# A DLRM interaction tower on one core: 27-vector products in two visits a step, and a second table of 1,250 rows on chip

## What is computed

```python
e = stack([tbl_f[ids[:, f]] for f in range(26)], axis=1)
combined = concatenate([dense[:, None, :], e], axis=1)
interactions = einsum('bnd,bmd->bnm', combined, combined)[:, TRIU_I, TRIU_J]
h = concatenate([dense, interactions, dense], axis=1)
h = maximum(h @ W_top1 + b_top1, 0.0)
h = maximum(h @ W_top2 + b_top2, 0.0)
y = h @ W_top3
```

## Time and profile before

| | us |
|---|---|
| median of 3 runs | 372.38 |
| lowest and highest | 370.5, 372.94 |
| span of the profiled execution | 373.1 |
| PE busy in it | 332.0 (89%) |
| PE weight loads busy | 298.5 (80%) |
| POOL busy | 258.6 (69%) |
| DVE busy, ACT busy | 207.1, 188.8 |

### The profile page before, as it was taken

The page is one execution under the profiler, slowest core; times in us unless marked ns, Lnnn a source line. Parts: engine busy times, 40 slices in busy tenths (PEclk is TensorE's granted clock), DMA queues, the critical chain, the costliest instruction groups (busy, mean ns, idle before and its releaser), DMA issues.

```text
span 373.1 us, 13491 instructions
## 1 busy us (share of the span) xinstructions
PE 332.0 (89%) x6048; PEld 298.5 (80%) x6048; DVE 207.1 (55%) x375; ACT 188.8 (51%) x223; POOL 258.6 (69%) x280
## 2 busy tenths in 40 slices
PE   0377859899999899998999999999999999999895
PEld 0377848898799778996789978998799878997685
DVE  3799745694089703874059912885079704860030
ACT  2698462455545473553635564554645563556402
POOL 6777777777777777777777777777777777776000
PEclk9997898899999999998999999999999999999999
DMA  7999426772226622464215722464226622442230
GB/s 178 246 259 212 135 79 174 193 229 69 55 68 151 198 53 59 95 194 125 58 54 128 233 54 58 93 192 131 58 59 150 205 54 57 105 116 62 51 40 21
DMA packets 49332, 44.24 MB, mean 119 GB/s; under 512 B 33359, under 2 KB 39094, under 8 KB 49274
## 3 DMA queue, kind: packets, MB, share of 16 engines
q1 hardware_dynamic: 39166, 25.36, 26.9%
q0 software_dynamic: 8704, 17.84, 18.2%
q10 hardware_dynamic: 1404, 0.17, 0.3%
HBM read 37.91 MB, written 5.44 MB: 116 GB/s over the span
## 4 chain that ended last, share of the span: by engine, by line
PE 82%; DMA 5%; issue 5%; ACT 4%; DVE 2%; SPq 1%; ACTq 1%; DVEq 0%
PE banks L443 38%; PE banks L462 14%; PE mlp L481 13%; PE moved L426 8%; PE mlp L491 7%; DMA w_sb<-in_tbl_dram 3%; DVE masks L672 1%; ACT vectors L818 1%; ACT hidden L846 1%; PE mlp L502 1%; SPq L250 1%; ACTq L229 1%; DMA scratch<-products 1%; DMA features<-scratch 1%; DVE low L659 1%
## 5 line engine op out<-in xcount | busy, mean ns | idle before, releaser
L401 POOL DMA_INDIRECT rows<-in_tbl_dram,ids_sb x272 | 257.7, 948 | 84.0 <-issue 80.8
L672 DVE TENSOR_TENSOR masks<-hot_ids,row_of 125x512 fp32r<-125x512 int32 (+1 forms) x336 | 185.6, 619 | 93.7 <-PE banks L443 84.8
L443 PE MATMUL banks<-masks,high 125*128 125x256 f32 x592 | 154.3, 298 | 17.4 <-DVE low L659 17.4
L443 PE MATMUL banks<-masks,low 125*128 125x256 f32 x592 | 150.3, 291 | 0.0
L443 PEld LDWEIGHTS banks<-masks,high 125*128 125x128 f32 x592 | 118.9, 201 | 18.1 <-issue 15.2
L443 PEld LDWEIGHTS banks<-masks,low 125*128 125x128 f32 x592 | 119.1, 201 | 0.0
L818 ACT ACTIVATE vectors<-moved 128x512 f32<-128x512 f32 (+1 forms) x80 | 86.8, 1085 | 4.6 <-PE moved L426 4.3
L801 ACT ACTIVATE vectors<-banks 128x512 f32<-128x512 f32 (+1 forms) x40 | 44.4, 1111 | 77.4 <-PE banks L443 77.4
L462 PEld LDWEIGHTS banks<-vectors 128*27 128x27 f32 x4096 | 44.5, 104 | 24.7 <-issue 19.6
L462 PE MATMUL banks<-vectors 128*27 128x27 f32 x4096 | 54.1, 193 | 9.7 <-issue 5.0
L481 PE MATMUL mlp<-features,w_sb 117*128 117x256 f32 x224 | 54.6, 388 | 0.0
(11 more groups left out here) (46 smaller groups left out, 64.4 us busy)
## 6 DMA issues: line engine op xcount, KB each, us to landing
hot_ids<-in_ids_of_field_dram SPq DMA_DIRECT2D x32, 256.0 KB, 4.9
rows<-in_tbl_dram,ids_sb POOLq DMA_INDIRECT x272
features<-scratch SPq DMA_DIRECT2D x7, 351.0 KB
scratch<-products SPq DMA_DIRECT2D x56, 42.2 KB
scratch<-products SPq DMA_DIRECT2D x28, 81.2 KB
w_sb<-in_tbl_dram SPq DMA_DIRECT2D x3, 448.0 KB
hot_ids<-in_ids_of_field_dram SPq DMA_DIRECT2D x8, 128.0 KB
dense_sb<-in_dense_dram SPq DMA_DIRECT2D x8, 128.0 KB, 5.2
```

The costliest lines, as they stand in the source:

```text
L401: pool.indirect_dma_start(rows[:, (tile * TILE_ROWS + v) % RING, :], None, tables[f][:, :], bass.IndirectOffsetOnAxis(ap=ids_sb[:, tile, f ...
L443: last = nc.tensor.matmul(banks[:, j % BANKS, m * CHUNK:(m + 1) * CHUNK], part[:, part_of(j * PAIR + m, k), :], masks[:, mask % MASK_RING, ...
L672: nc.vector.tensor_tensor(masks[:, mask % MASK_RING, 0:size], hot_ids[0:PART_ROWS, n % ID_RING, 0:size], row_of[0:PART_ROWS, row:row + 1]. ...
```

## The change

**Two visits a step.** The 64 matmuls of a `multiply` step are done as two groups of 32 with other work between them, in all steps but the first two of chunk 0 and the last of chunk 7. In `end_of_chunk` the first step's second group comes after the second `first_layer`, and the second step is spread around the third `first_layer` and the fourth turn; the `keep_step` calls on ScalarE move with them. The third and the fourth step are laced with the first look-up of the next chunk.

**A second table of 1,250 rows.** Field 3 (`SOMETIMES`) is put on chip too. In chunks 5 and 7 it is looked up, as the second table of the pair j = 4; in the other six chunks it is gathered as before, as the batch of one row. So chunks 5 and 7 have 16 gathers a tile and no fifth batch. Its table has its own staging buffer, `last_table`, loaded on SP after the ids. It is rounded, copied and split after the other nine (`round_table(HOT)`, `copy_table(HOT)`, `split(HOT)`).

```diff
+LOOKED_UP = (5, 7)
+ONE_HOT = [SOMETIMES, ALWAYS] + SHORTS
+STAGED = SHORTS + [ALWAYS, SOMETIMES]
...
+def batches_of(t):
+    return TILE_BATCHES - (t // TILES in LOOKED_UP)
+def fields_of(c, j):
+    if j < HOT_PAIRS - 1:
+        return (PAIR * j, PAIR * j + 1)
+    return (HOT, HOT - 1) if c in LOOKED_UP else (HOT - 1,)
...
             load_ids(1, slice(TILES, ALL_TILES))
+            load_table(HOT)
...
-                for b in range(TILE_BATCHES):
+                for b in range(batches_of(tile)):
                     gather(tile, b)
...
+            def multiply(c, s, visits=range(VISITS)):
+                for visit in visits:
+                    multiply_part(c, s, visit)
...
-                for g in range(STEP_GROUPS):
+                for g in range(visit * VISIT_GROUPS, (visit + 1) * VISIT_GROUPS):
...
-                last.then_inc(step_ready, 1)
+                if visit == VISITS - 1:
+                    last.then_inc(step_ready, 1)
...
             def end():
-                multiply(LAST, 2)
-                second_layer(LAST - 1, 1)
+                multiply(LAST, 2, (0,))
+                second_layer(LAST - 1, 1, range(0, 2))
+                multiply(LAST, 2, (1,))
+                second_layer(LAST - 1, 1, range(2, MTILES1))
                 multiply(LAST, 3)
...
             def end_of_chunk(i):
                 first_layer(i - 1, 0)
-                multiply(i, 0)
+                multiply(i, 0, (0,))
                 turn(b, 0)
                 first_layer(i - 1, 1)
-                multiply(i, 1)
+                multiply(i, 0, (1,))
                 turn(b, 1)
                 first_layer(i - 1, 2)
+                multiply(i, 1, (0,))
                 turn(b, 2)
                 first_layer(i - 1, 3)
                 turn(b, 3)
+                multiply(i, 1, (1,))
                 second_layer(i - 1, 0)
                 turn(b, 4)
                 if i < LAST:
                     second_layer(i - 1, 1)
-                    multiply(i, 2)
-                    look_up(i + 1, 0)
-                    multiply(i, 3)
+                    multiply(i, 2, (0,))
+                    look_up(i + 1, 0, range(0, 3))
+                    multiply(i, 2, (1,))
+                    look_up(i + 1, 0, range(3, 5))
+                    multiply(i, 3, (0,))
+                    look_up(i + 1, 0, range(5, PARTS[0]))
+                    multiply(i, 3, (1,))
...
@@ VectorE
             make_masks(0, HOT_PAIRS - 1)
+            split(HOT)
             place_dense(0)
...
@@ ScalarE, first_chunk
                 keep_batch(1, 1)
+                round_table(HOT)
+                copy_table(HOT)
                 keep_step(0, 0)
...
@@ ScalarE, end_of_chunk
                 keep_first(i - 1, 0)
-                keep_step(i, 0)
                 keep_batch(b, 0)
                 keep_first(i - 1, 1)
-                keep_step(i, 1)
+                keep_step(i, 0)
                 keep_batch(b, 1)
                 keep_first(i - 1, 2)
                 keep_batch(b, 2)
                 keep_first(i - 1, 3)
                 keep_batch(b, 3)
+                keep_step(i, 1)
                 keep_second(i - 1, 0)
```

More of the change, by code:

```diff
@@ L11 @@
 SHORT, LONG = 1000, 1250
-LONGS = [f for f in range(FIELDS) if ROWS[f] == LONG][:1]
-ONE_HOT = [f for f in range(FIELDS) if ROWS[f] == SHORT] + LONGS
+SHORTS = [f for f in range(FIELDS) if ROWS[f] == SHORT]
+ALWAYS, SOMETIMES = [f for f in range(FIELDS) if ROWS[f] == LONG][:2]
+LOOKED_UP = (5, 7)
+ONE_HOT = [SOMETIMES, ALWAYS] + SHORTS
+STAGED = SHORTS + [ALWAYS, SOMETIMES]
 GATHERED = [f for f in range(FIELDS) if f not in ONE_HOT]
@@ L36 @@
 CHUNK_STEPS = TILES * TILE_STEPS
+VISITS = 2
+VISIT_GROUPS = STEP_GROUPS // VISITS
 BATCH_SIZES = (4, 4, 4, 4, 1)
-TILE_ROWS = len(GATHERED)
+TILE_ROWS = len(GATHERED) + 1
 TILE_BATCHES = len(BATCH_SIZES)
-assert sum(BATCH_SIZES) == TILE_ROWS
+assert sum(BATCH_SIZES) == TILE_ROWS and BATCH_SIZES[-1] == 1
 CHUNK_BATCHES = TILES * TILE_BATCHES
@@ L50 @@
 PAIR = BANK // CHUNK
-HOT = len(ONE_HOT)
+HOT = len(STAGED) - 1
 HOT_PAIRS = -(-HOT // PAIR)
 WIDTHS = [min(PAIR, HOT - PAIR * j) for j in range(HOT_PAIRS)]
-PARTS = [ROWS[ONE_HOT[PAIR * j]] // PART_ROWS for j in range(HOT_PAIRS)]
+PARTS = [ROWS[STAGED[PAIR * j]] // PART_ROWS for j in range(HOT_PAIRS)]
 FIRST_PART = [sum(WIDTHS[n] * PARTS[n] for n in range(j)) for j in range(HOT_PAIRS + 1)]
@@ L64 @@
 assert CHUNK_STEPS == BANKS
[L65 removed]
+KINDS = [ROWS[SHORT_] // PART_ROWS for SHORT_ in (STAGED[0], STAGED[-1])]
 HIDDEN1, HIDDEN2 = 512, 256
@@ L85, with batches_before, rows_before @@
 SCRATCH_DMAS = QUAD_DMAS * QUADS
+def batches_of(t):
+    return TILE_BATCHES - (t // TILES in LOOKED_UP)
+def batches_before(t):
+    return sum(batches_of(n) for n in range(t))
+def rows_before(t):
+    return sum(TILE_ROWS - (n // TILES in LOOKED_UP) for n in range(t))
+def fields_of(c, j):
+    if j < HOT_PAIRS - 1:
+        return (PAIR * j, PAIR * j + 1)
+    return (HOT, HOT - 1) if c in LOOKED_UP else (HOT - 1,)
 def tile_batch(b):
@@ L94, in batch_of_row @@
 def batch_of_row(g):
-    tile, v = divmod(g, TILE_ROWS)
-    return tile * TILE_BATCHES + max(b for b in range(TILE_BATCHES) if tile_batch(b)[0] <= v)
+    tile = max(t for t in range(ALL_TILES) if rows_before(t) <= g)
+    v = g - rows_before(tile)
+    return batches_before(tile) + max(b for b in range(TILE_BATCHES) if tile_batch(b)[0] <= v)
 def part_of(h, k):
@@ L170, in build @@
         dense_loaded = [sem(f"dense_loaded{n}") for n in range(2)]
-        table_loaded = [sem(f"table_loaded{n}") for n in range(HOT)]
+        table_loaded = [sem(f"table_loaded{n}") for n in range(HOT + 1)]
         weights_loaded = sem("weights_loaded")
@@ L419, in turn @@
                     return
-                n = t * TILE_BATCHES + b
+                if b >= batches_of(t):
+                    return
+                n = batches_before(t) + b
                 batch = tile_batch(b)
-                pe.wait_ge(rows_loaded[t % TILES * TILE_BATCHES + b], (t // TILES + 1) * 16 * len(batch))
+                loads = sum(b < batches_of(n) for n in range(t % TILES, t + 1, TILES))
+                pe.wait_ge(rows_loaded[t % TILES * TILE_BATCHES + b], loads * 16 * len(batch))
                 if n:
@@ L426, in turn, with look_up @@
                     last = nc.tensor.transpose(moved[:, m * TILE:(m + 1) * TILE],
-                                               rows[:, (t * TILE_ROWS + v) % RING, :], identity[:, :])
+                                               rows[:, (rows_before(t) + v) % RING, :], identity[:, :])
                 last.then_inc(batch_ready, 1)
-            def look_up(c, j):
+            def look_up(c, j, ks=None):
+                ks = ks or range(PARTS[j])
+                if c == min(LOOKED_UP) and j == HOT_PAIRS - 1:
+                    pe.wait_ge(low_made, HOT + 1)
@@ L431, in look_up @@
                 if c == 0:
                     pe.wait_ge(low_made, PAIR * j + WIDTHS[j])
-                elif j < BANKS:
+                elif j < BANKS and ks[0] == 0:
                     pe.wait_ge(step_kept, (c - 1) * CHUNK_STEPS + j + 1)
-                if j >= BANKS:
+                if j >= BANKS and ks[0] == 0:
                     pe.wait_ge(pair_kept, c * HOT_PAIRS + j - BANKS + 1)
-                for k in range(PARTS[j]):
+                for k in ks:
                     mask = c * MASKS + FIRST_MASK[j] + k
@@ L440, in look_up @@
                     pe.wait_ge(mask_made, mask + 1)
-                    for m in range(WIDTHS[j]):
+                    fields = fields_of(c, j)
+                    for m, h in enumerate(fields):
                         for part in (high, low):
-                            last = nc.tensor.matmul(banks[:, j % BANKS, m * CHUNK:(m + 1) * CHUNK], part[:, part_of(j * PAIR + m, k), :],
+                            last = nc.tensor.matmul(banks[:, j % BANKS, m * CHUNK:(m + 1) * CHUNK], part[:, part_of(h, k), :],
@@ L489, in second_layer @@
                     pe.wait_ge(first_kept, MTILES1 * (c + 1))
-                for k in range(MTILES1):
+                for k in ks:
                     last = nc.tensor.matmul(mlp[:, m, 0:CHUNK], w2_sb[:, k, m * 128:(m + 1) * 128], hidden1[:, k, :],
                                             start=(k == 0), stop=(k == MTILES1 - 1))
-                last.then_inc(second_ready, 1)
+                if MTILES1 - 1 in ks:
+                    last.then_inc(second_ready, 1)
             def last_layer(c):
@@ L593, in first_chunk @@
                 turn(1, 4)
-                multiply(0, 2)
-                look_up(1, 0)
-                multiply(0, 3)
+                multiply(0, 2, (0,))
+                look_up(1, 0, range(0, 3))
+                multiply(0, 2, (1,))
+                look_up(1, 0, range(3, 5))
+                multiply(0, 3, (0,))
+                look_up(1, 0, range(5, PARTS[0]))
+                multiply(0, 3, (1,))
             def second_chunk():
```

50 lines of the change are left out of this document (30 added, 20 removed).

## The result

| | before | changed |
|---|---|---|
| median of 4 runs, us | 371.44 | 378.12 |
| lowest and highest | 370.31, 372.94 | 375.39, 379.35 |
| span of the profiled execution | 373.1 | 377.0 |

The ratio is 1.0187, with a 95% interval of 1.013 to 1.0243: the change makes the kernel 1.9% slower, 6.7 us, where 1% faster was forecast.

The account below looks back on a forecast made before the run. TensorE was taken to bound, GpSimd 2.7 us behind. 346.1 + 5.0 + 4.3 - 9.1 - 6.6 = 339.7, taken as 340.8, plus a tail of 28.2 made 369.0, or 368.3 us in the runs; range 365.8 to 373.0.

Parts of the forecast that it names:

- Start: Chunk 0: first products wait behind the tenth table's copy and split and the dense vectors' placement, +5.0 us.
- Look-ups: Chunks 5 and 7: twenty more matmuls in each, +4.8 us together; four one-row turns go, -0.5.
- Gathers: GpSimd: four gathers go, 5.0 us; the last starts at 337.4 and its rows are there at 339.7.
- The cause of the long pauses: TensorE: instructions come too late when a step uses up a 16 KB packet of 256 in under 3 us.
- Tail (+1.2): Last turn of four to the end: 28.2 us for 27.0, with some 3 us waiting for the first half's load.
- Long pauses (-6.6): TensorE's four long pauses and the lost clock, 8.3 us, shrink to 1.7 because packets last longer.
- Visits and waits for ScalarE (-9.1): Seven chunks at -1.3 us: -0.4 from steps in two groups, -0.9 from two waits for ScalarE that go.
- GpSimd's limit: Before the last turn of four: gathers stand 2.7 us behind TensorE, and after the change allow that turn at 339.7.
- The base: The profiled span was taken as 0.7 us above the runs' median, turning 369.0 into 368.3 us.
- number 4: Changes between dense work and products: more small groups cost more than they save, end 383 to 389.8 us; chance 0.10.
- Number 3: TensorE's long pauses stay, wholly or by half: end 370.4 to 373.7, in the runs about 371.5 us; chance 0.31.
- rival 1: The forecast itself: GpSimd and TensorE meet and the tail takes a new wait, 367 to 370 us; chance 0.45.

Follow-up runs that it names:

- e15: The changed kernel itself, unaltered, measured and profiled again: 378.31 us, ratio 1.015 to the kernel before.
- e10: The kernel before with the gathers of chunks 2 to 7 left out: 359.3 us, one execution.
- e5: The kernel before, unchanged, profiled a second time: 370.5 us, span 368.7.
- e9: The changed kernel with 44 unread transposes put into TensorE's idle time in the tail: 375.12 us, ratio 1.0071 to the kernel before.
- e11: e6 with the gathers of chunks 2 to 7 left out: 359.0 us, one execution.
- e6: The kernel before with products in two visits, no second table, the last chunk's closing part in the old order: 373.84 us, ratio 1.0046.
- e2: The kernel before with only the second table and its look-ups in chunks 5 and 7, products in the old order: ratio 1.0242, from two executions.
- e7: The changed kernel with the tenth table's split moved behind chunk 1's first masks and the last chunk's closing part in the old order: 371.22 us, ratio 0.9967.
- e13: The changed kernel with ScalarE's six second-half writes held until the first half's twelve have landed: 378.3 us, ratio 1.0134 to the kernel before.
- e1: The kernel before with only the products in two visits, no second table: 377.08 us, ratio 1.0137.

## Why the prediction was wrong

Right, in its place and its reason:
- **Start.** The chain is the one forecast, with 5.4 us of idle time. Against the profile shown the first layer is 3.1 and 2.3 late (84.1 to 87.2 and 86.4), against the second one 5.4 and 4.6 (81.8). Over all profiles it is at 83.0 in the eleven without that wait and at 88.2 in the six with it: 5.2, for +5.0 forecast.
- **Look-ups.** A chunk with one takes 42.3 for 40.1 in e15, +2.2 as forecast (43.2 and 42.8 in the changed kernel's first profile).
- **Gathers.** Four less, the last at 337.73 (forecast 337.4).
- **The cause of the long pauses.** The packet of 256 instructions that the prediction inferred fits every one of them (e10).

Wrong. Span for span, against the very execution that the sum started from, 369.0 was forecast and 377.0 came. Of these 8.0 us the tail has 4.7 (32.9 for 28.2) and the last turn of four 3.3 (344.1 for 340.8). Two steps failed: the tail's wait was taken as 3 us with 0.8 for the clock, and -9.1 and -6.6 were more than the visits give.
- **Tail (+1.2).** The mechanism was named, its size was too small: the tail grew by 5.9 against the profile shown and by 7.3 against e5. SP could write from +2.8 (forecast 2.6), issued for 6.0 (5.2), loaded 2.9 behind that (1.2), and the load took 2.8 (2.5): 14.6 for 11.8. TensorE had finished at +8.8, so it waited 5.9 and not 3. The clock took 2.7 (up to 1.5 allowed, 0.8 counted) [e9].
- **Long pauses (-6.6).** The sum let the first of the four shrink with the others, 1.8 and 1.4 for the clock behind it. The changed kernel still has 1.84 at that place (70.14), and the clock at 0.50 from 71.1 to 74.5. The other three have gone. And they aren't a fixed cost of the kernel before: e5 has 2.7 us of them and no dip of the clock behind one.
- **Visits and waits for ScalarE (-9.1).** From the first layer to the last turn the changed kernel gains 5.1 on the profile shown (262.0 to 256.9), where the terms give 8.2 (4.3 - 9.1 - 3.4; the first pause lies ahead). From chunk 1's mark to chunk 7's (six chunks) it is 246.3 and 245.5 in the changed kernel, 248.5 in e5. With 4.5 for two look-ups off and e5's two long pauses (2.15) off, the rest is 241.8 against 246.3, or 241.0: -0.75 to -0.9 a chunk, not -1.3. Left out was what the pieces of a look-up cost between groups, 0.37 a chunk; and e10 and e11 show that the visits are a cost of 0.5 to 0.85 which the pauses dodged pay back.
- **GpSimd's limit.** I had 2.7 us of margin; rows come 2.64 behind the gather's start, which leaves 2.3 in the execution shown, and nothing in e5. So visits alone (e6) bring no time. Gathers had to go for them to be worth anything, and the table that removes them costs about 9 us by itself (e2).
- **The base.** "The span was 0.7 above the median" set times of two kinds side by side. With the 1.9 us between span and time, the same sum of 369.0 is a run of 370.9: no change against 371.44, where 1% faster was forecast.

The rivals: number 4 had a grain of truth (more groups cost, 0.5 to 0.85 a chunk), but the pauses dodged outweigh it. Number 3 was right about the first pause alone. The kernel is slower for none of the four, which had 0.10 for slower: the start's wait was in the sum, and the tail's stood in rival 1 at half its size. From e5, 368.7: start +5, look-ups +4.5, visits -5.6 (7 chunks at 0.8), long pauses and the wait for rows -2.7, tail +7.3 make 377.2; the span was 377.0. The terms are read from the same profiles, so this is bookkeeping and no test.

The rule on changes of tiling mode ("TensorEngine Tiling (Array Packing)", "Key Properties", in the Trainium skill) fits the 0.33 of idle time ahead of a group behind dense work; that the drain is what fills it, no row shows. What eight groups cost over four is 0.55 us a chunk in the products (5.35 for 4.8), so the rule speaks against the change in sign, at 0.14 us for each of the four added groups.

## What to carry to other kernels

Before summing gains from one profile, tie its span to the runs: pauses that an execution has above the median are no gain, and one that stands where the change doesn't reach is none either. Two profiles of the kernel before were 4.4 us apart, more than the effect forecast. When work is moved to smooth the middle, follow the last chunk by itself: what feeds the tail's round trip through memory must stay early there, and a special order for the last chunk costs a few lines. Where two engines run level, relieving one alone brings nothing, and the relief has to come a chunk before the work that pays for it.

## What was not expected of the hardware

- A gather that GpSimd issues stops TensorE's small matmuls for 0.29 us, and without gathers the stops are gone (e10).
- TensorE's long pauses stand exactly 256 of its instructions apart or a multiple of it, waits counted in: 54 of 54. Which of the 750 places get one changes from execution to execution (three in e5 where the earlier trace rows has four).
- An idle TensorE costs twice: 5.9 us without work and then 10.3 us at 1.2 GHz. Work that nobody needs, put into the wait, gave 2.7 us back (e9).
- Twelve small writes from SP are through 1.2 us behind the last issue in e7 and 2.8 to 2.9 in the changed kernel and in e13. Neither ScalarE's writes (e13) nor the late start alone (e1: 1.35) is the reason. This stays open.
